# Cross-attention block with MLP on one core: the last two batches as a written-out program

## The reference, cut to what matters

```
q = layer_norm(x, ln1) @ q_w + q_b;  k = ctx @ k_w + k_b;  v = ctx @ v_w + v_b
attn = softmax(mask(q k^T / sqrt(32)))
hidden = (attn v) @ cproj_w + cproj_b + x
y = gelu_tanh(layer_norm(hidden, ln2) @ fc_w + fc_b) @ proj_w + proj_b
out = hidden + y
```

## Time and profile before

| | us |
|---|---|
| three timed runs | 746.65, 748.35, 753.88; median 748.35 |
| the profiled execution, device time | 742.84 |
| its span, first to last instruction | 741.0 |
| PE busy in it | 691.2 |
| DVE, ACT, POOL busy | 447.9, 314.0, 256.8 |

### The profile page before, as it was taken

One profiled execution on the slowest core, in us unless ns is written; L12 is line 12 of the kernel. 1 busy time (PEld: TensorE's weight loads), 2 busy tenths in 40 slices (PEclk: granted clock), 3 DMA queues, 4 the chain that ended last, 5 costly groups with the idle time before them and its releaser, 6 DMA issues.

```text
span 741.0 us, 13152 instructions
## 1 busy us (share of the span) xinstructions
PE 691.2 (93%) x4544; PEld 600.0 (81%) x4544; DVE 447.9 (60%) x867; ACT 314.0 (42%) x590; POOL 256.8 (35%) x222
## 2 busy tenths in 40 slices
PE   4578989999999999995789999999999999999998
PEld 3468889999989999994668888888888888888886
DVE  5367999898989798878668663522325322242113
ACT  4146776777787776765821212112111112111110
POOL 6108575757567574748614111000000110000000
PEclk9797999999999999999899999999999999999999
DMA  8674565646546464548009000100001000010001
GB/s 228 157 229 152 144 182 145 181 137 187 162 151 193 124 190 109 168 117 244 2 0 293 7 1 0 58 1 1 1 1 57 0 0 0 0 58 0 1 0 58
DMA packets 51152, 69.23 MB, mean 93 GB/s; under 512 B 8344, under 2 KB 29208, under 8 KB 51104
## 3 DMA queue, kind: packets, MB, share of 16 engines
q1 hardware_dynamic: 50832, 68.07, 31.5%
q0 software_dynamic: 272, 0.54, 0.4%
HBM read 47.21 MB, written 20.99 MB: 92 GB/s over the span
## 4 chain that ended last, share of the span: by engine, by line
PE 84%; DVE 4%; POOL 3%; issue 3%; ACT 2%; DMA 2%; SPq 1%; ACTq 0%; POOLq 0%; DVEq 0%
PE psum L1394 8%; PE psum L1396 8%; PE psum L1395 8%; PE psum L1381 8%; PE psum L1380 8%; PE psum L1379 8%; PE psum L1156 8%; PE psum L1157 7%; PE psum L1158 7%; PE psum L1188 4%; PE psum L1173 3%; POOL p_lo L503 2%; PE psum L1274 2%; PE psum L1239 2%; PE psum L1276 1%
## 5 line engine op out<-in xcount | busy, mean ns | idle before, releaser
L503 POOL TENSOR_TENSOR p_lo<-p,p_hi 128x512 f16<-128x512 f32 x128 | 154.3, 1209 | 104.0 <-ACT p_hi L628 104.0
L769 ACT ACTIVATE h<-psum,cols 128x512 f32<-128x512 f32 x64 | 44.1, 690 | 290.2 <-PE psum L1381 290.1
L1084 DVE CAST h_hi<-h 128x512 fp32r<-128x512 f32 x64 | 27.8, 435 | 208.2 <-ACT h L769 208.2
L1394 PE MATMUL psum<-w_mlp,h_hi 128*128 128x512 f32 x256 | 100.8, 394 | 0.9 <-DVE hidden L890 0.9
L1396 PE MATMUL psum<-w_mlp,h_lo 128*128 128x512 f32 x256 | 99.8, 390 | 0.0
L1395 PE MATMUL psum<-w_mlp,h_hi 128*128 128x512 f32 x256 | 99.7, 389 | 0.0
L1379 PE MATMUL psum<-y_hi,w_mlp 128*128 128x512 f32 x256 | 99.7, 389 | 0.0
L1381 PE MATMUL psum<-y_hi,w_mlp 128*128 128x512 f32 x256 | 99.6, 389 | 0.0
L1380 PE MATMUL psum<-y_lo,w_mlp 128*128 128x512 f32 x256 | 99.6, 389 | 0.0
L626 ACT ACTIVATE p<-psum,maskbias 128x512 f32<-128x512 f32 x128 | 87.2, 681 | 21.9 <-PE psum L1173 18.5
L628 ACT ACTIVATE p_hi<-psum,maskbias 128x512 f16<-128x512 f32 x128 | 87.5, 684 | 0.2 <-PE psum L1276 0.2
(11 more groups left out here) (105 smaller groups left out, 1507.5 us busy)
## 6 DMA issues: line engine op xcount, KB each, us to landing
qk_rows<-qk SPq DMA_DIRECT2D x32, 512.0 KB, 2.9
stacks<-qk_rows SPq DMA_DIRECT2D x64, 256.0 KB
stacks<-qk_rows SPq DMA_DIRECT2D x64, 128.0 KB
hidden<-in_x_dram SPq DMA_DIRECT2D x8, 512.0 KB, 4.0
ctx_sb<-in_ctx_dram SPq DMA_DIRECT2D x8, 512.0 KB, 5.2
w_mlp_raw<-in_L_xattn_fc_w_dram SPq DMA_DIRECT2D x16, 256.0 KB, 4.9
w_mlp_raw<-in_L_xattn_proj_w_dram SPq DMA_DIRECT2D x16, 256.0 KB, 6.7
out_dram<-hidden SPq DMA_DIRECT2D x16, 256.0 KB, 2.1
```

The costliest lines, as they stand in the source:

```text
L503: pool.tensor_tensor(p_lo[:, slot, :], p32[:, u % 2, :], p_hi[:, slot, :], ALU.subtract).then_inc(s["p_lo_done"], 1)
L1394: nc.tensor.matmul(acc, h_hi[:, f % 2, cut], w_mlp[f][:, 2, :], start=(f == 0), stop=False)
```

## The change

1. `iterations(eng, begin, step, end)`: the steps for it = -2 to 1 and it = 6 to 9 are replaced by lists `begin` and `end` that name every piece with its absolute number. `begin` has the pieces in the order that before's steps gave. The loop is as it was. `end` has another order.
2. On SP, the first six MLP weight tiles stood together behind the last `fill_stacks`; in `end` the two last `store_maxima` stand among them, behind tile 0 and behind tile 2.
3. The MLP accumulators are banks 0, 1, 4, 5 (before 0, 1, 6, 7); `transpose_y` uses 6 and 7 (before 4 and 5). `proj(0)` waits for `pv_taken`, no longer for `hidden_added`.
4. `h_hi` and `h_lo` lie at A1, in the stacks, and weight tile 8 where they were.
5. In `end` stand also `fc` 0 to 6 and `proj` 0 to 5 of the first chunk with their `gelu`, `split_h`, `weights` 0 to 9, and a small activation that loads the gelu table. The chunk's body starts at i = 6.
6. In the first chunk the transposes of the next one stand at i = 8, 10, 12, 14 (`turning`), their stats one body earlier and their norm in the same body, behind `split_h(i+1)`.
7. Names of semaphores, and `project_k` as a piece of its own for group 0; the bank's wait is looked up in the lists.

```diff
-        ACC, FC, TR = (0, 1, 6, 7), 2, 4
+        ACC, FC, TR = (0, 1, 4, 5), 2, 6
+        def turning(first):
+            return (8, 10, 12, 14) if first else (3, 6, 9, 12)
-            for it in range(-2, 2):
-                step(it, it % 2)
+            begin()
             with eng.Fori(1, B // 2 - 1) as pair:
                 for q in range(2):
                     step(pair * 2 + q, q)
-            for it in range(B - 2, B + 2):
-                step(it, it % 2)
+            end()
```

SP:

```diff
+            def end():
+                store_qk(0, 27); store_maxima(0, 25); fill_stacks(0, 27)
+                store_qk(0, 28); store_maxima(0, 26); fill_stacks(0, 28)
+                store_qk(0, 29); store_maxima(0, 27); fill_stacks(0, 29)
+                store_qk(0, 30); fill_stacks(0, 30); store_maxima(0, 28)
+                store_qk(0, 31); store_maxima(0, 29); fill_stacks(0, 31); load_tile(0); store_maxima(0, 30); load_tile(1); load_tile(2)
+                store_maxima(0, 31); load_tile(3); load_tile(4); load_tile(5); load_pb(); load_tile(6); load_tile(7); load_tile(8)
...
```

PE (the first number of a call is always 0; `values(0, 0, G, t)`):

```diff
+            def end():
+                scores(0, 26, 0); values(0, 0, 23, 0); transposed_scores(0, 24, 0); scores(0, 26, 1); transpose_ctx(0, 7, 0)
+                transposed_scores(0, 24, 1); values(0, 0, 23, 1); scores(0, 26, 2); transposed_scores(0, 24, 2); scores(0, 26, 3)
+                project_qk(0, 27); transposed_scores(0, 24, 3); transpose_max(0, 25); transpose_ctx(0, 7, 1); project_c(0, 4, 1)
+                transposed_scores(0, 25, 0)
+                project_qk(0, 28); transposed_scores(0, 25, 1); values(0, 0, 24, 0); scores(0, 27, 0); transpose_att(0, 5, 0)
...
+                project_qk(0, 30); transposed_scores(0, 27, 0); project_v(0, 7, 1); transposed_scores(0, 27, 1); scores(0, 29, 0)
+                values(0, 0, 26, 0); scores(0, 29, 1); transposed_scores(0, 27, 2); transpose_max(0, 28); scores(0, 29, 2)
+                values(0, 0, 26, 1); transposed_scores(0, 27, 3); scores(0, 29, 3)
+                project_qk(0, 31); transposed_scores(0, 28, 0); scores(0, 30, 0); transposed_scores(0, 28, 1); values(0, 0, 27, 0)
+                scores(0, 30, 1); values(0, 0, 27, 1); scores(0, 30, 2); transpose_max(0, 29); transposed_scores(0, 28, 2)
+                transposed_scores(0, 28, 3); scores(0, 30, 3); project_c(0, 5, 0); project_c(0, 5, 1); transposed_scores(0, 29, 0)
+                transpose_max(0, 30); transposed_scores(0, 29, 1); scores(0, 31, 0); transpose_att(0, 6, 0); values(0, 0, 28, 0)
+                transposed_scores(0, 29, 2); values(0, 0, 28, 1); scores(0, 31, 1); transpose_att(0, 6, 1); transposed_scores(0, 29, 3)
+                scores(0, 31, 2); transpose_y(0, 0, 0); transposed_scores(0, 30, 0); scores(0, 31, 3); transposed_scores(0, 30, 1)
+                transposed_scores(0, 30, 2); values(0, 0, 29, 0); values(0, 0, 29, 1); transposed_scores(0, 30, 3); transpose_max(0, 31)
+                transpose_y(0, 1, 1); transposed_scores(0, 31, 0); transpose_y(0, 2, 2); transposed_scores(0, 31, 1)
+                values(0, 0, 30, 0); values(0, 0, 30, 1); transposed_scores(0, 31, 2); project_c(0, 6, 0); transposed_scores(0, 31, 3)
+                transpose_y(0, 3, 3); values(0, 0, 31, 0); values(0, 0, 31, 1); project_c(0, 6, 1); transpose_att(0, 7, 0); fc(0, 0, 0)
+                transpose_att(0, 7, 1); fc(0, 1, 1); fc(0, 2, 2); project_c(0, 7, 0); project_c(0, 7, 1); proj(0, 0, 0); proj(0, 1, 1)
+                proj(0, 2, 2); fc(0, 3, 3); fc(0, 4, 4); fc(0, 5, 5); proj(0, 3, 3); proj(0, 4, 4); proj(0, 5, 5); fc(0, 6, 6)
             def body(c, first):
-                for i in range(FT):
-                    if i < FT - 1 and not (first and i == 0):
+                for i in range(6 if first else 0, FT):
+                    if i < FT - 1:
                         fc(c, c * FT + (i + 1), i + 1)
-                    if has_next(c) and i % 3 == 0 and 3 <= i <= 12:
-                        t = i // 3 - 1
+                    if has_next(c) and i in turning(first):
+                        t = turning(first).index(i)
                         transpose_y(c + 1, c * CH + (CH + t), t)
                     proj(c, c * FT + i, i)
```

ACT, the last part of `end`, and DVE, the last part of `end` and the chunk's body:

```diff
+                exps(0, 29, 0); attention_hi(0, 6, 0); exps(0, 29, 1); maxima_out(0, 30); attention_hi(0, 6, 1); exps(0, 29, 2)
+                exps(0, 29, 3); exps(0, 30, 0); exps(0, 30, 1); affine(0, 0, 0); maxima_out(0, 31); exps(0, 30, 2); exps(0, 30, 3)
+                affine(0, 1, 1); exps(0, 31, 0); exps(0, 31, 1); affine(0, 2, 2); exps(0, 31, 2); exps(0, 31, 3); affine(0, 3, 3)
...
+                split_y(0, 3); attention_lo(0, 7, 0); weights(2); attention_lo(0, 7, 1); split_h(0, 0); split_h(1, 1); weights(3)
+                add_hidden(0, 7, 0); weights(4); add_hidden(0, 7, 1); split_h(2, 2); weights(5); weights(6); weights(7); weights(8)
+                split_h(3, 3); split_h(4, 4); split_h(5, 5); split_h(6, 6); weights(9)
             def body(c, first):
-                for i in range(FT):
+                for i in range(6 if first else 0, FT):
                     if first and i + 4 < FT:
                         weights(i + 4)
                     if i < FT - 1:
                         split_h(c * FT + (i + 1), i + 1)
...
                     if has_next(c):
                         for t in range(CH):
-                            if i == 3 * t + 1:
+                            if i == turning(first)[t] - (1 if first else 2):
                                 ln2_stats(c * CH + (CH + t))
-                            if i == 3 * t + 2:
+                            if i == turning(first)[t] - (0 if first else 1):
                                 ln2_norm(c * CH + (CH + t), t)
```

737 lines of the change are left out of this document (403 added, 334 removed), and 14 rows, old and new, of tables (BEGIN, END).

## The result

| | before | after |
|---|---|---|
| median of 4 timed runs each, us | 750.9 | 765.3 |
| lowest to highest, us | 746.7 to 753.9 | 762.8 to 771.9 |
| profiled execution, device time / span, us | 742.84 / 741.0 | 764.11 / 762.3 |
| from the first scores of group 25 to proj(0), us | 104.0 | 113.1 |
| from proj(0) to the last matmul, us | 348.3 | 358.5 |

The ratio of the medians is 1.021 (95% interval 1.012 to 1.030). That the change is slower is clear; that it is slower by a full 2% is not. The forecast was 759.6, with 749 to 768. Executions of the kernels with the attention loop, the one before too, fall mostly into two clusters some 8 us apart.

The account below looks back on a forecast made before the run. It took PE's pace to bound the kernel, except 50.3 us before proj(0) with some 20 us to win. End -0.8, transposes +10.4 and clock +1.7 gave +11.3 on the 748.35 median: 759.6 us, range 749 to 768.

Parts of the forecast that it names:

- Begin and loop: Up to the loop's end: same pieces in the same order on every engine, so nothing, between -1 and +1 us.
- Stall for group 26: Right after the loop: PE's scores(26,0) waits for the five DMAs of group 26, 3.5 to 4.6 us, taken as 4.2.
- Stall for group 27: Before scores(27,0): too little PE work to cover group 27's fill, 3.1 to 3.8 us, taken as 3.3.
- "c(5,1) done": State in the end, at 338.8 before, reached at 346.9: stalls of 4.2, 3.3 and 1.2, less 0.6 of covered idle time.
- From there to proj(0): From c(5,1) done to the first proj: a chain of 40.7 us against before's 53.0 with fc(2), 12.3 won.
- The clock in the end: Two fill stalls and a thin stretch on ACT's chain may lower the clock: 0 to 5.1 us, two falls taken, 3.4.
- End in sum: The end up to proj(0): +8.1 for stalls, -12.3 for the chain, +3.4 for the clock, together -0.8 us.
- The transposes: First chunk, bodies 8, 10, 12, 14: PE waits for gelu, split and norm, 4 x 2.6 = 10.4 us.
- The clock there, one fall: First chunk, at the four transpose stalls: 0 to 6.8 us of clock loss, one fall taken, 1.7 us.
- Clock falls at every one: Rival: the clock falls at every new stall, +18.1 us, 766.5 us; chance 0.2.
- Planned end holds: Rival: fills of groups 26 and 27 land in time, release under 7 us, clock full: -1.3, 747.0 us; chance 0.1.
- The clock stays full: Rival: the clock stays full at all new stalls, +6.2 us, 754.5 us; chance 0.2.

Follow-up runs that it names:

- the clean pair above: Changed kernel against the kernel before, both with the attention loop written out: 764.2 against 743.3 us on the same chip.
- the run with both edits: Changed kernel with the next chunk's norm one body earlier and the start of the end list as before: 751.1 us, 1.001 against the kernel before.
- the old head: Changed kernel with PE, ACT and DVE in before's order for the first ten us behind the loop: 770.6 us, 1.024 against the kernel before.
- the store put back: Changed kernel with the stores of maxima of groups 30 and 31 behind weight tiles 0 to 5 again: 777.2 us, 1.037 against the kernel before.
- The new head alone: Changed kernel, order of the end and norm put back, loop written out, but scores(26) ahead of project_qk(27) as in the changed kernel's first ten us: 752.1 us.
- order and norm put back: Changed kernel with before's order of the end pieces up to project_c(6), norm one body earlier, loop written out: 741.9 us.

## Why the prediction was right, and where it was off

Direction, range and the deciding mechanism (the transposes) were right. The likeliest value was 5.7 us low; 765.3 lies in the band that had a chance of 0.2, not in the 755 to 763 that had 0.45. Against the clean pair above (+20.9) the sum of +11.3 was 9.6 low, and part of why the time still came out in the range is luck: the base of 748.35 lies 5 us above what the kernel before takes without the stop in the loop (742.84 in its profile, 743.3 with the loop written out), and that made up for half of the gap. By its own steps, with the profiles of before and after:

- **Begin and loop, nothing.** Not contradicted. The first scores of group 25 come 2.0 us later after the change (285.1, 287.1), but 0.2 earlier in the run with both edits, which has the same `begin`; 1.1 later in the pair without the loop. Two kernels with the same program up to there differ by 3.0.
- **Stall for group 26, 4.2 us.** 3.3. The chain was right: the lower of my two counts, from SP's last issue, gave 3.5.
- **Stall for group 27, 3.3.** Not as such. PE was held up for 1.7 by `transpose_max(25)`, whose bank the projection of group 27 still held until `low_parts`; that gave the DMAs time. The other waits for a fill are short (2.2 in all, three times).
- **"c(5,1) done" later by 8.1.** 12.3 (60.7 against 48.4). With the clock at 0.92 over 60.7 us, 4.9 of these are the clock, which the prediction had in a term of its own; 7.4 are stalls, against 8.1 in the sum. The sum of the stalls came out right, its parts did not: 3.3 and 1.7 us instead of 4.2 and 3.3, and the rest in short waits that the prediction had put at 1.2.
- **From there to proj(0), 40.7 against 53.0, -12.3.** This is the term that was mis-sized: 46.9, so -6.1. The last exponential ended 23.7 us behind `project_c(5,1)`, not 20.3: `scores(31,0)` waited 1.2 for its fill, ACT stood 1.0 for the transposed scores of group 31 and 0.5 in two other places, and an `affine` took 1.5 instead of 1.4. From there 23.2 us, not 20.4 (whose PE term, 5 x 2.7 + 0.4, is 13.9 and not 14.1). The chain in my sum was one in which every engine finds its input ready and PE's clock is full. The `project_c(6,1)` at 380.28 started at the lower clock, `add_hidden` (L950) came after it and two splits of y on DVE, and the transpose of att waited 1.6 us for that bank. Those splits ran while POOL normalised, and all took longer than elsewhere (timeline rows of POOL and DVE):

```profile
381.23 2.60 POOL L542 TENSOR_TENSOR att<-att,rl 128x512 f32<-128x512 f32 x2 [3.01 <-DVE rl L1050]
381.50 1.42 DVE L1141 TENSOR_TENSOR y_lo<-y_t,y_hi 128x512 fp32r<-128x512 f32 x1
382.85 1.27 DVE L1139 CAST y_hi<-y_t 128x512 fp32r<-128x512 f32 x1
```

The splits beside them take 0.69 and 0.42, and in the old order the two `normalise` take 2.06. It is so in all six profiles with the new order behind the last exponential, and in none of the seven with the old one, where DVE is done with its splits before POOL normalises. The 1.6 us more on DVE are as long as PE's wait for `add_hidden`; that the overlap is the reason was not tried by moving one of them.
- **The clock in the end, +3.4.** From the windows: 0.08 x 113.1 = 9.0 us lost after, 0.05 x 104.0 = 5.2 before; +3.8. The size is right as a difference, but it was added to a chain of durations at full clock that was set against a measured 53.0 us, which has before's 5 us of low clock in it (0.10 x 50.3). That booked their loss as won. After the change the same stretch lost 3.3 (0.07 x 46.9). It should have been: the new end has the falls of before, and new ones.
- **End in sum, -0.8.** +6.4 (113.1 - 106.7).
- **DVE's weights and `split_h`, 0 to 2.** 0.5 (the wait for `h_lo`).
- **The transposes, 4 x 2.6 = 10.4.** 9.7, four times, 2.4 each, at the lower bound. Moving the norm took all of them away. The first chunk took 94.0 us against 83.8 - 2.7 = 81.1: 12.9 more, 10.4 + 1.7 forecast.
- **The clock there, one fall.** One, at 488; the windows on either side of its start:

```profile
484.40:487.80 3.40, 1.42 (x8) 1.25 (x9) 1.58 (x3) 1.00 (x4) 1.29 (x1) 0.99 0.00 0
487.80:491.20 3.40, 3.40 (x9) 2.65 (x8) 2.49 (x5) 0.78 (x3) 0.00 (x0) 0.51 0.03 5
```

Four equal stalls of 2.4 us brought one fall here and in the changed kernel without the loop (0.02 x 94.0 = 1.9 us lost in the first chunk). With the old head, and with the store put back, the same four stalls brought two (0.04 x 94.0 = 3.8). So one fall, the prediction's choice, is a likely value and no fixed one. The Trainium skill's rule on depth-cycling ("TensorE: Matmul & The Clock Gate", section "A second HAM failure mode: psum-queue depth-cycling") says that frequent short idle times between groups of matmuls make the clock oscillate; taken for each of the four, that would be four falls, and the traces bear out one or two.

**What the end loses** is shown to be the new order on the five engines, with the banks of the first `transpose_y`: putting it back takes 113.0 to 105.2. The loss isn't the sum of its parts. The new head alone costs 9.4 us in the old order, the new rest alone 7.8 (113.0 against 105.2), and both together 7.9 (113.1 against 105.2). Whichever is there, the stretch comes out at 111.4 to 115.9 in six profiles (117.3 with the stores put back); with neither it is 105.2 or 105.3. Of the new rest, the loss lies ahead of the last exponential: from the first scores of group 25 to its end it takes 89.8 us in the new order and 80.1 in the old one, and behind it the new order is 1.9 shorter (23.2 against 25.1). Which piece does it stays open; no single wait of that kernel is longer than 2.9 us. Nor has the clock been held fixed in any run, so how much of a stall's price is the clock's is read from windows, and not shown by an experiment.

**The rivals.** "Clock falls at every one" gave 766.5, nearest to the 765.3 measured, but not by its mechanism: there was no fall at three of the transposes. "Planned end holds" decided on a release within 7 us; it came 10.2 us after group 26's `qk_high` (285.68 to 295.89), so that one is out. "The clock stays full" is out too (0.92). That the maxima of group 31 would be late behind two tiles is out too: 0.6 us. The stores among the tiles were the one part of the change for which a gain is seen: 4.2 us in the new order, where taking them back brings back one wait of that length; in the old order it is not settled.

**The lowest median** is that of the kernel before with the loop written out and those stores: 739.9 us, 1.1% under the kernel before on its chip (0.989, 0.984 to 0.994). Nothing else of the change is in it. It isn't told apart from the changed kernel with order and norm put back, 741.9 us and 0.993 (0.990 to 0.996) on another chip.

## What to carry to other kernels

When a new order is costed as a chain of durations, compare it with the old order as a chain of durations, not with the old order's measured time, which has lower clock and small waits in it; otherwise the difference between a model and a measurement is booked as a gain. In a stage where PE has no slack, look for an instruction that was put behind one that waits for PE: there, it costs its whole chain each time. And a stall that is refilled by another bound costs little to remove and much to add, so price each edit on top of the order in which it will stay. And take more than one profile of the same program before reading a difference: here one such stretch moved by up to 3 us, as much as several of the edits were worth.

## What the runs showed of the hardware

- **A jump back can cost about 9 us, in some executions.** With the loop, 25 runs of the kernel before on one chip lie at 742.5 to 746.4 (9 runs) and at 752.2 to 754.9 (16). On another chip the two clusters are less clean: 21 runs lie from 742.5 to 757.4, three of them between 749.0 and 751.9. Without the loop, 44 runs of five kernels lie 2.6 to 5.9 us apart in each. Four profiles show the stop, 4.8 to 6.4 us of "issue" at the first matmul behind the jump, and the lower clock behind it; they have 37 packets on the queue of instructions where the four without it have 28. The Trainium skill, "Runtime: NRT & Kernel Launch", section "Instruction fetch mechanics", says that a taken branch whose target isn't among the pages held forces a fetch before execution goes on. The rows fit that; why the same program pays it in some executions only, no run shows.
- **A stall can cost nearly its own length again in clock, but at no fixed rate.** In the head alone, 5.2 us more of idle time came with 4.2 us more of PE at work for the same matmuls. At the jump 6.4 us of idle time came with 2.6, and four stalls of 9.7 us together came with 1.9 in two profiles and 3.8 in two others.
- **A small store waits behind large copies.** In the kernel before without the loop, the 12 KB store of the maxima was issued at 345.11, behind twelve weight copies, and released PE at 350.53, 5.4 us later. In the changed kernel group 30's store, with one tile ahead of it, was issued at 358.45 and its reader ran at 360.73, 2.3 us later and without waiting for it; with the store put back behind the six tiles it was 366.22 to 371.80, 5.6 us. The prediction had counted 2.6 for a free queue, from no row that it shows.
- **DVE and POOL took longer side by side.** While the two `normalise` ran on POOL, two splits of y on DVE took 1.42 and 1.27 us instead of 0.69 and 0.42, and the `normalise` 2.60 instead of 2.06, in six profiles of six.
